# Fetching 31 of 1563 gather tiles of one graph layer row by row on SyncE and ScalarE

## The chip, the cores and the metric

The kernel runs on one core of one Trainium2 chip. The metric is the device time of one execution in microseconds, less being better. The time before is the median of three runs.

## The reference

Four graph layers over 12,500 nodes with 128 features and 200,000 edges sorted by destination. Each layer ends in a layer norm. The change is in the third layer (called "sum" in the kernel):

```python
x = _layernorm(x + L0(x, edges))          # softmax over edges
x = _layernorm(x + L1(x, src, dst))       # four attention heads, MLP
# the third layer, L2:
deg  = segment_sum(ones_like(dst), dst)   # self loops included
dinv = rsqrt(deg)
h    = x @ W
msgs = h[src] * (dinv[src] * dinv[dst])[:, None]
out  = gelu(segment_sum(msgs, dst) + b)
x = _layernorm(x + out)
# the fourth, L3: messages from gelu([x[src], x[dst], w] @ We1 + be1) @ We2
x = _layernorm(x + L3(x, edges, edge_weight))
```

## The kernel before

The edges are cut into 1563 tiles of 128 edges. Four tiles make a group (391 groups) and 16 tiles a block `b`. Each layer is one pass over the tiles, followed by a pass over the nodes. `edge_soft` runs the first layer (its tiles are named `rows`, `frow_h`) and the second (`rows_h`). `edge_light` runs the third, with mode "sum" (`rows_sum`, `pn_sum`), and the fourth, with mode "mlp" (`rows_mlp`, `frow_mlp`).

A tile needs the 128 rows of a table in DRAM that its edges' sources name. The usual way is one indirect DMA on GpSimd (L581 in `edge_light`), which picks the 128 rows by a column of indices and puts one into each partition of `rows`. There are eight group slots in `rows` (`NR`), so GpSimd may be at most eight groups, 32 tiles, ahead of the tensor engine; for slot reuse it waits on `s_mm`, which the last matmul of a group raises.

In "sum" mode the tensor engine's `place(g)` clears a PSUM bank with a matmul of zeros (L627), waits for the group's one-hot matrices `S` and for its gathered rows, and multiplies each tile's rows with its one-hot matrix (L640), which adds the rows of equal destinations. VectorE makes the one-hots one group ahead (`hot`, L745) and adds the PSUM bank into the accumulator `big` (`add`, L772), waiting for `s_mm`. A bank is used again only after the add of the group two before (`s_add`). ScalarE has nothing to do in this pass. SyncE loads some weights, writes a list of row addresses (`far_d`, then `flist`), writes `deg`, and is then idle.

There is a second way to bring in a tile, used for a few of them and called a lane: 128 separate DMAs of one row each, with the address of each read from `flist` into a register (`load_values`, 16 rows at a time). They fill `frow`, which has three slots (`DEEP`). In "mlp" mode lane 1 brings in the last tile of every sixth block on the ScalarE queue, 15 tiles, six rows after each activation. The first layer brings in 14 tiles the same way on the SyncE queue, one tile's 128 rows in one go (`fetch` in `edge_soft`, L941). GpSimd skips such tiles (`continue`).

```python
lanes = ([], FETCHED[1] if mlp else [])
lane = {t: (q, k) for q, tiles in enumerate(lanes) for k, t in enumerate(tiles)}
```

so that in "sum" mode `lane` is empty and GpSimd gathers all 1563 tiles.

Of the kernel before, what the change touches and what calls it, by code (L numbers as in the profile page):

```python
# [23 lines left out]
P = 128  # L24
# [8 lines left out]
NB = 16  # L33
# [7 lines left out]
SIZE = [min(4, TILES - 4 * g) for g in range(GR)]  # L41
# [3 lines left out]
SEED = 1597463007.0  # L45
RING = 8
APART = 6
FETCHED = ([], [NB * b + NB - 1 for b in range(6, 96, APART)])
DEEP = 3
FETCHED0 = [NB * b + NB - 1 for b in range(9, 90, APART)]  # L50
W0, W1, XR = F + 1, H * DH + H + 1, F + 8
# [11 lines left out]
def prog(nc, a, out, stop=99, debug=False):  # L63
    kind = "ExternalOutput" if debug else "Internal"

    def dram(name, shape, dt):
        return nc.dram_tensor(name, shape, dt, kind=kind).ap()
# [14 lines left out]
    deg_d = dram("deg_d", (NT, 3, P), BF16)  # L82
    far_d = dram("far_d", (sum(map(len, FETCHED)), P), I32)
    lrn_d = dram("lrn_d", (NT, P), BF16)

    with ExitStack() as top:
        def sb(name, shape, dt=F32, ctx=top):
            return ctx.enter_context(nc.sbuf_tensor(name, shape, dt))
# [55 lines left out]
        if stop <= 3:  # L144
# [5 lines left out]
            ("one3", [3, P], BF16))}  # L150
        consts["flist"] = sb("flist", [33, max(map(len, FETCHED)) * P], I32)
        edge_light(nc, sb, "sum", t2_d, big, dict(consts, dn=dn, w=w, a=a), d)
# [300 lines left out]
def edge_light(nc, sb, mode, table, acc, c, d):  # L453

    mlp = mode == "mlp"
    NR, NS, ND, NW = RING, 4, 4, 2
    PE, DVE, SP = mybir.EngineType.PE, mybir.EngineType.DVE, mybir.EngineType.SP
    NQ = NB // 4

    with ExitStack() as ctx:  # L460
# [8 lines left out]

        rows = s("rows", [P, NR, 4, F])  # L470
        idx, lr, regs = c["idx"], c["lr"], c["regs"]
        lanes = ([], FETCHED[1] if mlp else [])
        lane = {t: (q, k) for q, tiles in enumerate(lanes) for k, t in enumerate(tiles)}
        S = s("S", [P, NS, 4, P])
        zb = s("zb", [P, 512], BF16)
# [2 lines left out]
        if mlp:  # L478
            lrb = s("lrb", [P, NW, EB], U8)
            w = s("w", [P, B, NB])  # L480
            crowb = s("crowb", [P, F])
            dw = s("dw", [P, ND, 4, F])
            ST = s("ST", [P, 2, 4, P])
            pre = [ps(f"pre{i}", [P, 4, P]) for i in range(2)]
            s_base = sem("s_base")
            s_edge = [sem(f"s_edge{i}") for i in range(NW)]
            s_dw = [sem(f"s_dw{i}") for i in range(ND)]
            s_st, s_ex, s_pre, s_gelu = sem("s_st"), sem("s_ex"), sem("s_pre"), sem("s_gelu")
        else:
            we2, we2T = s("we2", [P, F]), s("we2T", [P, F])  # L490
            be2, be9, betc, buc = s("be2", [P, 1]), s("be9", [P, 9]), s("betc", [P, 1]), s("buc", [P, 1])
            bu2, be3 = s("bu2", [3, F]), s("be3", [3, F])
            v9, v9r, v9p = s("v9", [9, F]), s("v9r", [9, F]), s("v9p", [9, 3, F], BF16)
            mask, degf, deg = s("mask", [9, 6]), s("degf", [NT, P]), s("deg", [NT, 3, P], BF16)
            pw = ps("pw", [P, 4, P])
            s_w, s_dd, s_p, s_pv = sem("s_w"), sem("s_dd"), sem("s_p"), sem("s_pv")
            many = [len(tiles) for tiles in FETCHED]
            fcol, fidx = s("fcol", [P, sum(many)]), s("fidx", [sum(many), P], I32)
            px = ps("px", [P, P])
            s_fx = sem("s_fx")  # L500
# [3 lines left out]
        s_g, landed = c["s_g"], list(c["landed"])  # L504
        s_init, s_S, s_mm, s_add = sem("s_init"), sem("s_S"), sem("s_mm"), sem("s_add")
        block = ctx.enter_context(nc.Block(no_gpsimd_drain=True))
# [6 lines left out]
        def rows_of(e, engine, q, k, p, n):  # L513

            r0 = load_values(nc, engine, flist[32 * q:32 * q + 1, k * P + p:k * P + p + n], N * F * 4)
            for i in range(n):
                e.dma_start(frow[q][p + i:p + i + 1, k % DEEP, :].bitcast(U8), byte[:, bass.ds(r0[i], F * 4)]
                            ).then_inc(s_far[q][k % DEEP], 16)

        def gathered(g):  # L520
            return s_g[g % NR], landed[g % NR] + 16 * sum(near(k) for k in range(g % NR, g + 1, NR))
# [4 lines left out]
        @block.sync  # L526
        def _(e):
            if not mlp:
                a, wt = c["a"], c["w"]
                row = lambda n, k: a[n].rearrange("(o f) -> o f", o=1).broadcast_to([k, F])  # L530
                col = lambda n: a[n].rearrange("(p o) -> p o", o=1)
                e.dma_start(we2[:, :], a["L3_gnn_We2"]).then_inc(s_w, 16)
                e.dma_start(wt["wu"][:, :, :], a["L3_gnn_Wu1"].rearrange("(k p) j -> p k j", p=P)).then_inc(s_w, 16)
                e.dma_start(wt["we"][:, :, :], a["L3_gnn_We1"][0:2 * F, :].rearrange("(k p) j -> p k j", p=P)).then_inc(s_w, 16)
                e.dma_start(wt["wu2"][:, :], a["L3_gnn_Wu2"]).then_inc(s_w, 16)
                e.dma_start(wt["wg"][:, :], a["L2_gnn_W"]).then_inc(s_w, 16)
                e.dma_start(wt["bg"][:, :], row("L2_gnn_b", P)).then_inc(s_w, 16)
                for t, n in ((be2, "L3_gnn_be2"), (betc, "L3_gnn_beta"), (buc, "L3_gnn_bu1")):
                    e.dma_start(t[:, :], col(n), allow_slow_non_contiguous=True).then_inc(s_w, 16)
                for t, n, k in ((wt["be"], "L3_gnn_be1", P), (wt["bet"], "L3_gnn_beta", P), (wt["gam"], "L3_gnn_gamma", P),  # L540
                                (bu2, "L3_gnn_bu2", 3), (be3, "L3_gnn_beta", 3)):
                    e.dma_start(t[:, :], row(n, k)).then_inc(s_w, 16)
                e.wait_ge(s_fx, 3)
                e.dma_start(d["far"], fidx[:, :]).then_inc(s_dd, 16)
                e.wait_ge(s_dd, 16)
                for q in range(2):
                    if many[q]:
                        e.dma_start(flist[32 * q:32 * q + 1, 0:many[q] * P],
                                    d["far"][q * many[0]:q * many[0] + many[q], :].rearrange("t e -> (t e)").rearrange("(o x) -> o x", o=1)
                                    ).then_inc(s_dd, 16)  # L550
                listed = 16 + 16 * sum(n > 0 for n in many)
                e.wait_ge(s_dd, listed)
                e.wait_ge(s_pv, 3)
                e.dma_start(d["deg"], deg[:, :, :]).then_inc(s_dd, 16)
                e.wait_ge(s_dd, listed + 16)
                return
            e.dma_start(crowb[:, :], c["crow"].broadcast_to([P, F])).then_inc(s_base, 16)
            e.dma_start(w[:, :, :].rearrange("p b t -> p (b t)"), d["wcol"]).then_inc(s_base, 16)
            for g in range(GR):
                b, q = divmod(g, NQ)  # L560
                if q == 0:
                    if b >= NW:
                        e.wait_ge(s_ex, (b - NW + 1) * NQ)
                    e.dma_start(lrb[:, b % NW, :], d["lrrow"][b:b + 1, :].broadcast_to([P, EB])).then_inc(s_edge[b % NW], 16)
                    r0 = load_values(nc, SP, regs[BASE:BASE + 1, b * NB:(b + 1) * NB], N)
                if g >= ND:
                    e.wait_ge(s_ex, g - ND + 1)
                for j in range(SIZE[g]):
                    e.dma_start(dw[:, g % ND, j, :], d["dst"][bass.ds(r0[4 * q + j], P), :]).then_inc(s_dw[g % ND], 16)

        @block.gpsimd
        def _(e):
            for g in range(GR):
                if g >= NR:
                    e.wait_ge(s_mm, g - NR + 1)
                b, q = divmod(g, NQ)
                for j in range(SIZE[g]):
                    t = 4 * q + j
                    if 4 * g + j in lane:
                        continue  # L580
                    e.indirect_dma_start(rows[:, g % NR, j, :], None, table,  # L581
                                         bass.IndirectOffsetOnAxis(ap=idx[:, b, t:t + 1].bitcast(I32), axis=0)
                                         ).then_inc(s_g[g % NR], 16)

        if mlp:
            @block.scalar
# [72 lines left out]
        def _(e):  # L659
# [5 lines left out]
            e.memset(zb[:, :], 0.0)  # L665
            e.drain().then_inc(s_init, 1)
            if not mlp:
                for q in [q for q in range(2) if many[q]]:
                    f0, f1 = q * many[0], q * many[0] + many[q]
                    b0 = FETCHED[q][0] // NB  # L670
                    e.tensor_scalar(fcol[:, f0:f1], idx[:, b0:b0 + APART * (many[q] - 1) + 1:APART, NB - 1].bitcast(I32), float(F * 4), None, ALU.mult)
                e.drain().then_inc(s_fx, 1)
                e.wait_ge(s_fx, 2)
# [111 lines left out]
            for i in range(GR + lag):  # L785
# [8 lines left out]
                g = i - lag  # L794
# [5 lines left out]
                add(g, r0[g % 16])  # L800
            e.drain()

    for k in range(len(FETCHED[1]) if mlp else 0):
        c["far"][k % DEEP] += 16 * P
    for g in range(GR):
        c["landed"][g % NR] += 16 * sum(not mlp or 4 * g + j not in FETCHED[1] for j in range(SIZE[g]))


CHAIN = ("score", "scoreT", "scan1", "row1", "scanI", "col1", "scan2", "row2", "scanJ", "col2", "scan3", "exp",
# [1692 lines left out]
```

## Time and profile before

| | |
|---|---|
| median of 3 runs | 10216.46 us (10213.39 to 10222.34) |
| profiled execution, its own time | 10213.39 us |
| its span, first to last instruction | 10211.6 us |
| GpSimd (POOL) busy | 6159.7 us, 60% |
| TensorE matmul (PE) busy | 5172.9 us, 51% |
| VectorE (DVE) busy | 5157.6 us, 51% |
| ScalarE (ACT) busy | 2350.8 us, 23% |
| mean granted TensorE clock | 0.673 |

The span holds four edge passes one after the other, each with a node pass behind it. The pass that the change touches goes from the first gather into `rows_sum` at 5334.8 us to the last add into `big` at 7567.3 us. A share of the whole span therefore says little; what counts is what paces this pass.

### The profile page before, as it was taken

The page shows a single profiled execution, that of the slowest core. Times are in us where ns is not written, and L with a number is a line of the kernel's source. Part 1 is how long each engine was busy: PE and PEld are TensorE (multiplying, and loading weights), DVE is VectorE, ACT ScalarE, POOL GpSimd, SP SyncE. Part 2 cuts the span into 40 slices and gives each one's busy share as a digit, 9 for nine tenths or more (in the row PEclk, how much of TensorE's full clock was granted, in tenths as well). Part 3 has the DMA queues.
Part 4 walks back from the last instruction along what each step waited for, and adds up shares of the span by engine and source line. Part 5 has one row for each costly group of instructions (what it writes and reads, how often), then busy time and mean ns, then how long its engine had stood idle before and what let it go on. Part 6 is the DMA issues. An engine that isn't in the chain of part 4 may idle for free. (4 is left out here: it accounts for less than half of the span.)

```text
span 10211.6 us, 117807 instructions
## 1 busy us (share of the span) xinstructions
PE 5172.9 (51%) x26943; PEld 4434.7 (43%) x27385; DVE 5157.6 (51%) x11737; ACT 2350.8 (23%) x7991; POOL 6159.7 (60%) x6684
## 2 busy tenths in 40 slices
PE   1544444447365666666673323333345565666655
PEld 1434433435254555555552222222244555555553
DVE  4644544546466666666652222222245555555556
ACT  1212211224244444444460000000021111111114
POOL 5666666662566555555516666666656666666664
PEclk9556556667677777777786656555576766666677
DMA  4222222222444444444421111111123333333331
GB/s 110 46 46 47 46 46 46 47 46 86 100 101 99 99 98 98 98 98 98 99 68 47 46 47 46 47 46 46 46 62 109 100 101 101 102 100 102 101 100 43
DMA packets 869663, 769.76 MB, mean 75 GB/s; under 512 B 385028, under 2 KB 727929, under 8 KB 868606
## 3 DMA queue, kind: packets, MB, share of 16 engines
q0 software_dynamic: 230416, 528.66, 20.4%
q1 hardware_dynamic: 626235, 228.48, 9.4%
q10 hardware_dynamic: 12344, 5.06, 0.2%
q8 instruction: 255, 4.18, 0.2%
q14 instruction: 413, 3.38, 0.1%
HBM read 707.24 MB, written 54.30 MB: 75 GB/s over the span
## 5 line engine op out<-in xcount | busy, mean ns | idle before, releaser
L1007 POOL DMA_INDIRECT rows_h<-t_d,idx x1563 | 1482.3, 948 | 1024.9 <-issue 396.3
L581 POOL DMA_INDIRECT rows_sum<-t_d,idx x1563 | 1474.7, 944 | 962.8 <-issue 453.5
L581 POOL DMA_INDIRECT rows_mlp<-t_d,idx x1548 | 1468.7, 949 | 834.1 <-remote 419.0
L1007 POOL DMA_INDIRECT rows<-t_d,idx x1477 | 1396.7, 946 | 812.6 <-issue 409.7
L1152 PEld LDWEIGHTS pn_h<-S_h,rows_h 128*128 128x128 f32 x6252 | 1098.1, 260 | 258.5 <-issue 223.2
L1152 PE MATMUL pn_h<-S_h,rows_h 128*128 128x128 f32 x6252 | 1141.6, 348 | 124.8 <-issue 110.3
L1047 ACT ACTIVATE rows_h<-rows_h,wc_h 128x64 f32<-128x64 f32 x4688 | 1135.9, 334 | 17.1 <-issue 7.0
L772 DVE TENSOR_TENSOR big<-big,pn_sum 128x512 f32 x391 | 269.2, 689 | 1687.0 <-remote 1535.6
L620 PE MATMUL pre_mlp<-dw_mlp,ST_mlp 128*128 128x128 f32 x3126 | 674.5, 379 | 475.8 <-DVE ST_mlp L59 185.3
L627 PE MATMUL pn_sum<-zb_sum 128*128 128x512 bf16 x325 | 175.4, 540 | 1294.4 <-DVE big L772 1089.9
L620 PEld LDWEIGHTS pre_mlp<-dw_mlp,ST_mlp 128*128 128x128 f32 x3126 | 591.2, 280 | 528.5 <-issue 513.8
L1152 PE MATMUL pn_h<-S_h,rows 128*128 128x128 f32 x3126 | 736.3, 398 | 51.8 <-ACT rows L1047 20.5
L640 PE MATMUL pn_mlp<-S_mlp,rows_mlp 128*128 128x128 f32 x3126 | 664.6, 383 | 175.2 <-DVE big L772 96.1
L640 PE MATMUL pn_sum<-S_sum,rows_sum 128*128 128x128 f32 x3126 | 606.5, 358 | 236.1 <-DVE big L772 156.8
L591 ACT ACTIVATE rows_mlp<-rows_mlp 128x512 f32<-128x512 f32 x391 | 246.2, 630 | 2079.2 <-DVE rows_mlp L765 1335.3
L1152 PEld LDWEIGHTS pn_h<-S_h,rows 128*128 128x128 f32 x3126 | 683.6, 301 | 86.1 <-issue 44.9
L627 PEld LDWEIGHTS pn_sum<-zb_sum 128*128 128x128 bf16 x391 | 43.3, 111 | 1536.2 <-DVE big L772 1278.1
L640 PEld LDWEIGHTS pn_mlp<-S_mlp,rows_mlp 128*128 128x128 f32 x3126 | 655.7, 296 | 59.2 <-issue 14.6
L1161 PE MATMUL hist<-lo_h,ho_h 128*98 128x128 bf16 x1563 | 241.5, 305 | 771.1 <-DVE lo_h L1387 589.6
L640 PEld LDWEIGHTS pn_sum<-S_sum,rows_sum 128*128 128x128 f32 x3126 | 588.5, 271 | 66.7 <-issue 30.7
L772 DVE TENSOR_TENSOR big<-big,pn_mlp 128x512 f32 x391 | 269.1, 688 | 681.6 <-remote 629.6
L1463 DVE TENSOR_TENSOR acc<-acc,pn_h 128x512 f32 x391 | 269.4, 689 | 676.1 <-remote 521.9
(361 smaller groups left out, 8634.5 us busy)
## 6 DMA issues: line engine op xcount, KB each, us to landing
dw_mlp<-bd_d SPq DMA_DIRECT2D x1563, 64.0 KB
frow_mlp<-t_d ACTq DMA_DIRECT2D x1920, 0.5 KB
frow_h<-t_d SPq DMA_DIRECT2D x1792, 0.5 KB
lrb_h<-lrrow_d SPq DMA_DIRECT2D x196, 128.0 KB
lrb_mlp<-lrrow_d SPq DMA_DIRECT2D x98, 256.0 KB
rows_h<-t_d,idx POOLq DMA_INDIRECT x1563
dw_h<-xp_d SPq DMA_DIRECT2D x1563, 3.0 KB
rows_sum<-t_d,idx POOLq DMA_INDIRECT x1563
```

Of the source, the lines that this page charges most:

```text
L581: e.indirect_dma_start(rows[:, g % NR, j, :], None, table, bass.IndirectOffsetOnAxis(ap=idx[:, b, t:t + 1].bitcast(I32), axis=0)).then_inc ...
L591: e.activation(v, v, ACT.Gelu).then_inc(s_gelu, 1)
L620: last = e.matmul(pre[g % 2][:, j, :], ST[:, g % 2, j, :], dw[:, g % ND, j, :], start=True, stop=True)
L627: e.matmul(pn[g % 2][:, :], zb[:, 0:P], zb[:, :], start=True, stop=False)
L640: last = e.matmul(pn[g % 2][:, bass.ds(r0[j], P)], x, S[:, g % NS, j, :], start=False, stop=(j == SIZE[g] - 1))
L772: e.tensor_tensor(w, w, pn[g % 2][:, :], ALU.add).then_inc(s_add, 1)
L1007: e.indirect_dma_start(rows[:, g % NR, j, :], None, table, bass.IndirectOffsetOnAxis(ap=idx[:, b16, t:t + 1].bitcast(I32), axis=0)).then_i ...
L1047: last = e.activation(v, x, ACT.Copy, scale=wc[:, b % 2, t * heads + h:t * heads + h + 1])
L1152: last = e.matmul(pn[g % 2][:, k, bass.ds(r0, P)], rows[:, g % NR, j, k * P:(k + 1) * P], S[:, g % NS, j, :], start=False, stop=last_tile)
L1161: last = e.matmul(hist[:, :], ho[:, g % 2, j, :], lo[:, g % 2, j, :], start=False, stop=False)
L1463: e.tensor_tensor(w, w, pn[g % 2][:, :, :], ALU.add).then_inc(s_add, 1)
```

## The change

In "sum" mode 31 tiles leave GpSimd. Lane 0 (the last tile of blocks 3, 9, ..., 93, 16 tiles) is issued on the SyncE queue, lane 1 (blocks 6, 12, ..., 90, 15 tiles) on the ScalarE queue, each tile as 128 DMAs of one row. A lane issues its first three tiles without a wait, and from then on waits until the tile three before has been placed. In "mlp" mode lane 1 stays as it was. The list of addresses grows from 15 to 31 rows.

```diff
-FETCHED = ([], [NB * b + NB - 1 for b in range(6, 96, APART)])
+FETCHED = ([NB * b + NB - 1 for b in range(3, 96, APART)], [NB * b + NB - 1 for b in range(6, 96, APART)])
@@ edge_light
-        lanes = ([], FETCHED[1] if mlp else [])
+        lanes = ([], FETCHED[1]) if mlp else FETCHED
...
-            many = [len(tiles) for tiles in FETCHED]
+            many = [len(tiles) for tiles in lanes]
...
+        def fetch(e, engine, q):
+            for k, t in enumerate(lanes[q]):
+                if k >= DEEP:
+                    e.wait_ge(s_mm, lanes[q][k - DEEP] // 4 + 1)
+                for p in range(0, P, 16):
+                    rows_of(e, engine, q, k, p, 16)
@@ sync, after the weights, the list and deg
+                fetch(e, SP, 0)
@@ new
+        if not mlp and many[1]:
+            @block.scalar
+            def _(e):
+                e.wait_ge(s_dd, 48)
+                fetch(e, mybir.EngineType.Activation, 1)
@@ vector, the list of addresses
-                for q in [q for q in range(2) if many[q]]:
+                for q in range(2 if many[1] else 1):
...
-                    b0 = FETCHED[q][0] // NB
+                    b0 = lanes[q][0] // NB
@@ counts of landed DMAs for the later stages
-    for k in range(len(FETCHED[1]) if mlp else 0):
+    for k in range(0 if mlp else len(FETCHED[0])):
+        c["come"][k % DEEP] += 16 * P
+    for k in range(len(FETCHED[1])):
         c["far"][k % DEEP] += 16 * P
```

## Rows read from the trace of the kernel before

**Rows 1.** Span of the core, mean granted clock.

```profile
core 0: 10211.6 us, clock 0.673
```

**Rows 2.** Costliest groups: line, engine, operation, count, busy, mean ns, idle before, releaser.

```profile
L581 POOL DMA_INDIRECT rows_sum<-t_d,idx x1563 | 1474.7, 944 | 962.8 <-issue 453.5
L772 DVE TENSOR_TENSOR big<-big,pn_sum 128x512 f32 x391 | 269.2, 689 | 1687.0 <-remote 1535.6
```

**Rows 3.** Windows, sum and mlp pass: busy PE, PEld, DVE, ACT, POOL; clock, DMA share, GB/s.

```profile
5340.00:7550.00 2210.00, 683.54 (x3408) 610.71 (x3473) 505.27 (x812) 0.00 (x0) 1464.92 (x1553) 0.60 0.18 47
7700.00:9980.00 2280.00, 1365.77 (x6388) 1242.17 (x6516) 1320.01 (x3088) 241.31 (x383) 1453.25 (x1533) 0.67 0.38 101
```

**Rows 4.** The gather's line in the sum pass: durations, first and last start, idle before.

```profile
L581 POOL DMA_INDIRECT rows_sum<-t_d,idx x1563: 938/944/1061, 5334.8 to 7556.7; - x196
...
  issue: 453.5, 1478
  remote: 286.6, 75
```

**Rows 5.** Timeline of GpSimd: start, duration, idle before and its releaser.

```profile
5380.26 0.94 POOL L581 DMA_INDIRECT rows_sum<-t_d,idx  x1 [5.58 <-PE pn_sum L640]
...
6029.42 0.94 POOL L581 DMA_INDIRECT rows_sum<-t_d,idx  x1 [4.46 <-remote]
6030.67 0.94 POOL L581 DMA_INDIRECT rows_sum<-t_d,idx  x1 [0.30 <-issue]
```

**Rows 6.** GpSimd, mlp pass: tiles 87, 135, 183; then 1335, 1383, 1431.

```profile
7816.51 0.94 POOL L581 DMA_INDIRECT rows_mlp<-t_d,idx  x1 [0.30 <-issue]
...
7887.62 0.94 POOL L581 DMA_INDIRECT rows_mlp<-t_d,idx  x1 [0.30 <-issue]
...
7959.24 0.94 POOL L581 DMA_INDIRECT rows_mlp<-t_d,idx  x1 [0.30 <-issue]
...
9657.13 0.94 POOL L581 DMA_INDIRECT rows_mlp<-t_d,idx  x1 [0.30 <-issue]
...
9727.30 0.94 POOL L581 DMA_INDIRECT rows_mlp<-t_d,idx  x1 [0.30 <-issue]
...
9798.94 0.94 POOL L581 DMA_INDIRECT rows_mlp<-t_d,idx  x1 [0.30 <-issue]
```

**Rows 7.** SyncE's queue, first layer: one lane tile of 128 rows each.

```profile
406.78 85.15 SPq L941 DMA_DIRECT2D frow_h<-t_d  x128
...
1246.82 110.15 SPq L941 DMA_DIRECT2D frow_h<-t_d  x128
```

**Rows 8.** First layer's gathers in windows with and without SyncE issuing a lane tile.

```profile
1246.80:1356.00 109.20, 69.66 (x74) 0.61 0.21 46
1184.40:1246.80 62.40, 40.50 (x44) 0.58 0.21 47
1527.90:1634.10 106.20, 68.27 (x73) 0.61 0.21 46
1459.80:1527.90 68.10, 44.29 (x47) 0.58 0.21 47
```

**Rows 9.** SyncE's queue at the start of the sum pass.

```profile
5344.03 0.22 SPq L548 DMA_DIRECT2D flist<-far_d  x1
5349.22 0.31 SPq L554 DMA_DIRECT2D deg_d<-deg_sum  x1
```

**Rows 10.** Gather of tile 63, add of its group 15, first gather of group 23.

```profile
5423.14 0.94 POOL L581 DMA_INDIRECT rows_sum<-t_d,idx  x1 [0.30 <-issue]
...
5453.68 0.69 DVE L772 TENSOR_TENSOR big<-big,pn_sum 128x512 f32 x1 [0.73 <-issue]
...
5463.55 0.94 POOL L581 DMA_INDIRECT rows_sum<-t_d,idx  x1 [0.30 <-issue]
```

**Rows 11.** ScalarE around the sum pass, and its lane in the mlp pass.

```profile
7568.37 1.28 ACT L2148 ACT_TABLE_LOAD   x1 [2235.37 <-PEq L460]
...
7740.06 2.00 ACTq L517 DMA_DIRECT2D frow_mlp<-t_d  x6
```

More of the change, by code:

```diff
@@ L801, in _ @@
             e.drain()
-    for k in range(len(FETCHED[1]) if mlp else 0):
+    for k in range(0 if mlp else len(FETCHED[0])):
+        c["come"][k % DEEP] += 16 * P
+    for k in range(len(FETCHED[1])):
         c["far"][k % DEEP] += 16 * P
     for g in range(GR):
-        c["landed"][g % NR] += 16 * sum(not mlp or 4 * g + j not in FETCHED[1] for j in range(SIZE[g]))
+        c["landed"][g % NR] += 16 * sum(4 * g + j not in FETCHED[1] + ([] if mlp else FETCHED[0]) for j in range(SIZE[g]))
 CHAIN = ("score", "scoreT", "scan1", "row1", "scanI", "col1", "scan2", "row2", "scanJ", "col2", "scan3", "exp",
```

## The prediction

> **What bounds the kernel now.** I began with the span [rows 1] and the list of costliest groups [rows 2]. The largest are the indirect gathers of the four edge passes; that of the sum pass takes 944 ns of GpSimd each time. The change touches one pass only, so the share of the whole span is set aside and a window is laid over that pass [rows 3]: of 2210 us GpSimd is busy 1464.92, the matmuls 683.54, VectorE 505.27, ScalarE 0, and the DMA engines 0.18 of the time. Nothing in it is full. The DMA engines are not what is short: they move 47 GB/s here, and 101 GB/s in the mlp pass, which keeps GpSimd busy for nearly the same share [rows 3].
>
> The gather's own line [rows 4] gives the pace: first start 5334.8, last 7556.7, so (7556.7 - 5334.8) / 1562 = 1.4225 us from one to the next. It has two parts. Start to start inside a run of gathers is 1.25 us, as 6029.42 to 6030.67 shows [rows 5]: 0.94 busy and 0.30 that nothing else ends (1.249 in the mean over such pairs). The rest is pauses: 75 waits that another engine ended, 286.6 us together [rows 4], of the kind at 6029.42 with 4.46 us [rows 5]. They come mostly after 24 gathers: 24 x 1.249 = 29.97, plus 4.16 more than the usual 0.30, makes a cycle of about 34.2 us. The wait in the code at that place is the one for a free slot of `rows`, that is for `s_mm` of the group eight before. So the pass is paced by GpSimd's issuing for 88% of the time (1.249 / 1.4225), and for 12% GpSimd has run its ring full and waits for the tensor engine. VectorE is waiting at the same time: 1535.6 us idle before `big<-big,pn_sum` are put down to the same unknown releaser [rows 2]. The add of group 15 starts 5453.68 - 5423.14 = 30.5 us after the group's last gather [rows 10], though the matmuls of a group are busy for 683.54 / 391 = 1.75 us [rows 3]. The trace does not tell why the ring is used to its end by an engine that is busy a third of the time, and this is where I can be wrong.
>
> **The change part by part.** *Removed:* 31 gathers on GpSimd. Price of one: at least the 1.25 us of issue. At most the whole 1.4225 if its share of the pauses goes too. The mlp pass shows which is nearer, for it has lane tiles already. Between the gathers of tiles 87 and 135, with lane tile 111 among them, 71.11 us pass, and over the next 48 tiles, all gathered, 71.62. At the end of the pass, between tiles 1335 and 1383, with lane tile 1359 among them, 9727.30 - 9657.13 = 70.17; over the next 48, 9798.94 - 9727.30 = 71.64. These are the first and the last of 14 such pairs [rows 6], with means 70.17 and 71.43, a difference of 1.26. That is one issue, and the pauses stay as they are. Both kinds of window have the lane's DMAs running, so this is the gain without the lane's price. 31 x 1.249 = 38.7 us.
>
> *Added on the two queues:* 31 x 128 = 3968 row DMAs with their address registers, on SyncE and ScalarE. ScalarE is idle through the whole pass (2235.37 us before its next instruction, [rows 11]) and SyncE after 5349.22 [rows 9], so nothing is queued behind them there. What they may cost is felt by GpSimd or the tensor engine. The first layer shows such bursts: SyncE takes 85.15 us for a tile's 128 rows in one of the shortest of its 14 bursts and 110.15 in one of the longest, the first aside [rows 7]. In windows with a burst the gathers come every 109.20 / 74 = 1.476 and 106.20 / 73 = 1.455 us, in windows without one every 62.40 / 44 = 1.418 and 68.10 / 47 = 1.449 [rows 8]. The difference of the means, 1.465 - 1.434 = 0.031 us over the 70 gathers of a burst, would be 2.2 us per lane tile. This is an upper bound: the windows without a burst are the tail of a batch, where the softmax chain of that layer rests too. Lower bound: nothing, since the gathers of [rows 6] keep their 0.30 us of idle time although ScalarE issues rows in that pass, and the DMA share of 0.18 leaves room. I see no way to a gain from a burst. I take 0.25 us each, near the low end, because in this pass both issuing engines have nothing else to do and no chain is beside them: 31 x 0.25 = 7.8 us.
>
> The Trainium skill ("DMA: Bandwidth & Descriptors", Anatomy of one DMA) puts a fixed cost of about 2.0 us on each DMA, however small. If a lane paid that for each row in turn, a tile would take 128 x 2.0 = 256 us, as an estimate from that page, and the two lanes would be the bound of the pass. The bursts disagree as far as one lane goes: 85.15 / 128 = 0.67 and 110.15 / 128 = 0.86 us per row [rows 7], so the rows overlap in flight.
>
> *Can the lanes keep up?* Lane tiles of one lane are 96 tiles apart, and 96 tiles last 96 x 1.4225 = 136.6 us now, about 135 after the change. A burst takes 85 to 110. Both lanes run at once, which no stretch of this trace shows at full rate; ScalarE's six rows in 2.00 us [rows 11], issued while SyncE loads windows for the same pass, say that the two queues don't stand in line for each other. The tight one is the first: tile 63. SyncE can begin after 5349.22 + 0.31 [rows 9]; with 85 to 110 us it has issued the last row between 5435 and 5460, and the row lands a little later. VectorE adds its group now at 5453.68 [rows 10]. GpSimd asks for that group's slot at group 23, at 5463.55, so a tensor engine held until shortly after 5460 does not stop GpSimd: cost 0, and what is late beyond that is paid once. ScalarE's first, tile 111, has 48 tiles more to wait for, 68 us; the three slots put the others in time as long as a burst is under 135 us.
>
> *Added on VectorE and SyncE at the start:* one more small `tensor_scalar` for the list, and one more DMA for `flist` (0.22 us, [rows 9]). GpSimd stands still before its 33rd gather for 5.58 us until the first group's matmuls [rows 5], so VectorE's extra instruction goes straight into the path: about 0.3 us, from both sides between 0.1 and 1. I leave it out of the sum.
>
> *Moved:* nothing else. The waits of `place` on the lane's semaphore are new but met if the above holds; behind them stand the matmuls of the group, and behind those VectorE's add and GpSimd's slot.
>
> The sum: -38.7 + 7.8 = -31 us. Against the profiled execution's own 10213.4 us (span 10211.6, 1.8 around it) that is 10182.5; the median of the runs is 3.1 above that execution, so 10216.5 - 31 = 10185.5.
>
> **The rivals.** *The pauses take it back.* The tensor engine is a full ring behind, so it may be that some pace of its own, 34.2 us for six groups, rules the pass, and GpSimd only fills the time. For it: the 30.5 us of [rows 10], nearly the full ring, and VectorE's idle time. Against it: the pairs of [rows 6], where a ring of the same size paced GpSimd too. A cycle would stay at 34.2 us with 23 gathers and the pause 1.25 longer. Time 10216, no change.
>
> *The bursts cost more than a gather saves.* Place: the gather's pace, or the pause, while a lane issues. The lanes issue 31 x 97 = 3000 us in a pass of 2200, so somewhere a burst is always on. It decides from 1.25 us per burst, and is seen as slower from 1.9. At the 2.2 us from [rows 8]: 31 x 2.2 = 68, less 38.7, is 10246, slower. Against it: in [rows 8] the other work of the batch is mixed in.
>
> *The lanes are too slow together.* If two at once stretch a burst to 170 us, a lane needs 16 x 170 = 2720 us and the pass is 500 us longer. Stretched to 145, it is 16 x 145 = 2320 against 2190: 10290 or so. For it: a row DMA in [rows 7] takes two to three times the 0.33 us of [rows 11], so something already holds them up. Against it: 25 us to spare even at a long burst.
>
> *More than forecast:* a gather takes its share of the pause along and a burst is free. 31 x 1.4225 = 44 us: 10172. It lies in the same direction and is the low end.
>
> **How the numbers follow.** A difference of 0.2%, 20 us, is about what a measurement of this kernel can tell from none. The forecast with its own range (10170 to 10200) has 0.66, of which 0.03 stays within 20 us; pauses that take it back 0.17; costly bursts 0.12; slow lanes 0.05. That is faster 0.63, same 0.20, slower 0.17. The range goes from 10166, somewhat under the 44 us case, to 10232, which takes in the unchanged time and the lesser half of the costly bursts. It leaves out the slow lanes, the rest of the costly bursts, and 0.03 below.
>
> **What would show it.** 1532 gathers in `rows_sum` instead of 1563; start to start still 1.25 us; a cycle of six groups with a lane tile about 32.9 us long and one without 34.2; the sum of the pauses still near 280 us; last gather near 7526 instead of 7556.7; all other passes unchanged in length. If the pauses sum to 320 us, the first rival holds. If a lane's 128 rows take over 135 us and matmuls of `frow_sum` wait for DMAs, the lanes are too slow. If pauses grow in bursts only, it is their price. The weakest step is the 0.25 us; next to it that the rest of the ring behaves as in the mlp pass, whose pauses come after every 8 gathers and not after 24.

## The result: 0.9% slower

The median of the changed kernel is 10302.5 us (10276.5 to 10320.7) against 10212.8 us (10185.3 to 10222.3) for the kernel before, six runs each. The ratio is 1.0091 with a 95% interval of 1.007 to 1.011: 90 us slower by the medians, 93 (71 to 112) by the ratio. The prediction was 10185.5 us, 31 faster. The profiled execution took 10333.2 us itself, 31 above its median: the gathers of its first layer start at 158.4 us, those of the kernel before at 138.9. So lengths of passes are compared here and not their places in time.

The core's span, which answers to [rows 1], and the two groups that answer to [rows 2], from the list of costliest groups (columns as there; the gather's line is now L590, the add's L787):

```profile
core 0: 10331.4 us, clock 0.675
```

```profile
L590 POOL DMA_INDIRECT rows_sum<-t_d,idx x1532 | 1447.9, 945 | 1086.3 <-issue 432.3
...
L787 DVE TENSOR_TENSOR big<-big,pn_sum 128x512 f32 x391 | 269.2, 688 | 1779.9 <-remote 1369.7
```

The gathers are 31 fewer and 27 us less busy, and GpSimd's idle time before them grew by 124 us. A window over the pass (columns as in [rows 3]; this one is 90 us longer):

```profile
5360.00:7660.00 2300.00, 734.27 (x3400) 658.42 (x3464) 502.98 (x808) 0.00 (x0) 1436.20 (x1521) 0.60 0.17 45
```

GpSimd, VectorE and the DMA engines are no fuller than before, and the DMA engines move 45 GB/s where they moved 47: the rows are not short of bandwidth. The granted clock is 0.60 in both windows, so the clock is not the cause either. The gather's own line shows the pass and where the idle time went (it answers to [rows 4]; the row of POOLq is the stretch before the pass):

```profile
L590 POOL DMA_INDIRECT rows_sum<-t_d,idx x1532: 939/945/961, 5354.4 to 7672.8; - x192
...
  issue: 432.3, 1403
  remote: 321.8, 113
  POOLq L1812: 214.9, 1
  PE pn_sum L655: 117.3, 15
```

From first to last gather 2318.4 us pass, where it was 2221.9 [rows 4]: 96.5 longer. The last row is the one that grew. In the same view of the kernel before it was this:

```profile
  PE pn_sum L640: 8.0, 9
```

GpSimd waited 8.0 us for matmuls in this pass; now it waits 117.3, 15 times. What the matmuls wait for is seen at the lane's tiles, `frow_sum`:

```profile
L517 SPq DMA_DIRECT2D frow_sum<-t_d x2048: 2/228/1454, 5370.6 to 7625.8; - x187
L517 ACTq MOVE frow_sum<-t_d x1920: 3/29/1435, 5366.2 to 7254.6; - x192
L517 ACTq DMA_DIRECT2D frow_sum<-t_d x1920: 3/214/1417, 5366.3 to 7256.0; - x192
...
its engine sat idle before it (us, times) until:
  issue: 289.7, 17
  DMA frow_sum<-t_d: 262.6, 15
who waited for it (us, times):
  PE pn_sum L655: 274.1, 16
  DVE big L787: 197.7, 15
  POOL rows_sum L590: 109.6, 14
```

Fifteen times a matmul waits for a lane's rows, 262.6 us in all, and 109.6 us of that reach GpSimd through its ring of eight groups. The lane is SyncE's. In its timeline one row covers the whole pass, because nothing but row DMAs comes between:

```profile
5370.64 2255.89 SPq L517 DMA_DIRECT2D frow_sum<-t_d  x2048
```

That is 2255.89 / 16 = 141.0 us for a tile, against 85 to 110 in [rows 7] and the 135 to 137 that the pace allows. ScalarE's 15 tiles end at 7256.0, 417 us before the last gather, at 126 us each with its waits for slots.

The first of the waits is tile 63, the one that the prediction called tight. First the matmuls of its group, then GpSimd at group 23, in their timelines:

```profile
5469.80 0.50 PE L655 MATMUL pn_sum<-S_sum,rows_sum 128*128 128x128 f32 x3
5509.52 0.79 PE L655 MATMUL pn_sum<-S_sum,frow_sum 128*128 128x128 f32 x2 [39.23 <-DMA frow_sum<-t_d]
```

```profile
5510.58 0.94 POOL L590 DMA_INDIRECT rows_sum<-t_d,idx  x1 [26.01 <-PE pn_sum L655]
5511.83 0.94 POOL L590 DMA_INDIRECT rows_sum<-t_d,idx  x1 [0.31 <-issue]
```

The row arrives 139 us after SyncE began, and GpSimd stands for 26 us. Start to start after it is 1.25 us, as before. The passes around changed much less: from first to last gather 2490.1 us in the second layer (2503.8 before) and 2309.7 in the mlp pass (2300.7).

### The profile page after: what moved, and what is told of

Read it like the earlier page. It is cut to its first block and busy times, and to the rows that moved or that the text cites. A ratio compares the mean times of both kernels' runs of the same rounds, so it can differ in the third digit from the quotient of the medians.

```text
span 10331.4 us, 125962 instructions
## 1 busy us (share of the span) xinstructions
PE 5216.4 (50%) x26943; PEld 4473.0 (43%) x27385; DVE 5156.8 (50%) x11738; ACT 2353.7 (23%) x7991; POOL 6140.1 (59%) x6653
## 5 line engine op out<-in xcount | busy, mean ns | idle before, releaser
L590 POOL DMA_INDIRECT rows_sum<-t_d,idx x1532 | 1447.9, 945 | 1086.3 <-issue 432.3
L590 POOL DMA_INDIRECT rows_mlp<-t_d,idx x1548 | 1469.2, 949 | 842.5 <-remote 426.4
L787 DVE TENSOR_TENSOR big<-big,pn_sum 128x512 f32 x391 | 269.2, 688 | 1779.9 <-remote 1369.7
L655 PE MATMUL pn_sum<-S_sum,rows_sum 128*128 128x128 f32 x3064 | 632.2, 375 | 258.3 <-issue 126.1
L655 PEld LDWEIGHTS pn_sum<-S_sum,rows_sum 128*128 128x128 f32 x3064 | 626.5, 290 | 73.7 <-issue 31.5
L787 DVE TENSOR_TENSOR big<-big,pn_mlp 128x512 f32 x391 | 269.0, 688 | 678.3 <-remote 618.3
```

The costliest lines, as they stand in the source:

```text
L590: e.indirect_dma_start(rows[:, g % NR, j, :], None, table, bass.IndirectOffsetOnAxis(ap=idx[:, b, t:t + 1].bitcast(I32), axis=0)).then_inc ...
L655: last = e.matmul(pn[g % 2][:, bass.ds(r0[j], P)], x, S[:, g % NS, j, :], start=False, stop=(j == SIZE[g] - 1))
L787: e.tensor_tensor(w, w, pn[g % 2][:, :], ALU.add).then_inc(s_add, 1)
```

## The experiments

All stand against the kernel before on their own chip. In the tables, "idle" is the sum of GpSimd's three rows of idle time in this pass (issue, remote, matmuls of `pn_sum`), 748.1 us in the kernel before [rows 4, with 8.0 for the matmuls]. Each gather that is gone would take 0.305 us of it along (1.249 - 0.944); "more" is what is above that. "About us" is the difference from the kernel before: the ratio, less one, times its median. A "burst" is the 128 row DMAs of one lane tile.

How far can one trace's idle time be trusted? Two later runs, `mlp_plain` and `no_lanes`, leave this pass as it was, and have 750.3 and 746.4 us of it. In the mlp pass, which 13 of the traces share unchanged, it goes from 825.0 to 841.5. So "more" is good to some 5 us, and 24 us over 15 bursts is 1.6 us each, give or take 0.4.

### What the pieces cost: one lane, no lane, no use of the rows

`left_out`: the 31 tiles are neither gathered nor fetched (their matmuls read a cleared buffer, so their edges' messages are missing).

```diff
-                fetch(e, SP, 0)
-                fetch(e, mybir.EngineType.Activation, 1)
```

> The 31 tiles are neither gathered nor fetched: zeros stand in for their rows, so the third layer lacks these 3968 edges. What 31 gathers are worth with no price. Theories A and B: 31 x 1.25 to 1.42 = 39 to 44 us faster than before. Theory C: within 10 us of before, the pauses longer by 39 us in sum.

`act_only`: SyncE's lane empty, its tiles gathered. `sp_only`: the same for ScalarE's.

```diff
-        lanes = ([], FETCHED[1]) if mlp else FETCHED
+        lanes = ([], FETCHED[1])                     # act_only
+        lanes = ([], FETCHED[1]) if mlp else (FETCHED[0], [])   # sp_only
```

> ScalarE's lane alone: its 15 tiles are fetched row by row in the sum pass, the 16 of SyncE's lane are gathered again. Theory A (SyncE's lane is the bound: it needs some 141 us for a tile's 128 rows where its tiles are 96 x 1.42 = 137 us apart, and the gathers are not slowed): ScalarE's bursts of 97 to 132 us fit in, so 15 gathers at 1.25 us are saved, 19 us faster than before, about 10194. Theory B (each burst slows the gathers; the changed kernel's 90 us and the 39 us saved, over 31 tiles, make 4.2 us per burst): 15 x (4.2 - 1.25) = 44 us slower. Theory C (the pauses take back what is saved): no change.

> SyncE's lane alone: 16 tiles, ScalarE's 15 are gathered again. Theory A: as slow as both lanes if a burst still takes 141 us (16 x 141 + 55 us = 2311 us of pass against 2232, 75 to 95 us slower than before); if SyncE is slow only because ScalarE issues beside it, bursts fall to 100 us and the kernel is 20 us faster than before. Theory B: 16 x (4.2 - 1.25) = 47 us slower.

`rows_unused`: all 1563 tiles gathered, both lanes' 3968 row DMAs issued all the same.

```diff
-        lane = {t: (q, k) for q, tiles in enumerate(lanes) for k, t in enumerate(tiles)}
+        lane = {...the same...} if mlp else {}
+                    e.wait_ge(s_far[q][k % DEEP], before[q][k % DEEP] + 16 * P * (k // DEEP))
```

> All 1563 tiles are gathered, and both lanes' 3968 row DMAs are issued all the same; the tensor engine reads the gathered tiles and waits for no row. Price of the bursts alone. Theory A: the gathers keep their 1.42 us, first to last 2222 us; the pass ends only when SyncE has issued its last row, at some 16 x 141 us, 60 us later than before. Theory B: first to last gather takes 31 x 4.2 = 130 us more.

`act_unused`: `rows_unused` with ScalarE's lane alone.

> All 1563 tiles are gathered as before; ScalarE issues its 15 x 128 row DMAs all the same, and no one uses them; SyncE has none. This is the price of a burst by itself. At 1.5 us each the kernel is 15 x 1.5 = 22 us slower than before (+15 to +30) and the pauses of the pass are near 271.7 + 22 = 294 us. At the forecast's 0.25 us it would be +4 us, at 2.2 us +33.

| | gathers | bursts | ratio (95%) | about us | idle | more |
|---|---|---|---|---|---|---|
| left_out | 1532 | 0 | 0.996 (0.9945 to 0.9974) | -41 | 732.3 | -6 |
| act_only | 1548 | 15 | 1.0007 (0.9998 to 1.0016) | +7 | 766.0 | +22.5 |
| sp_only | 1547 | 16 | 1.0026 (1.0014 to 1.0038) | +27 | 783.4 | +40 |
| act_unused | 1563 | 15 | 1.0033 (1.0022 to 1.0044) | +34 | 772.2 | +24 |
| rows_unused | 1563 | 31 | 1.0199 (1.0173 to 1.0224) | +203 | 793.5 | +45 |
| changed kernel | 1532 | 31 | 1.0091 (1.007 to 1.011) | +93 | 871.4 | +133 |

The gathers are worth what was forecast, 41 us for 31. The price of a burst is not: 22.5 / 15 = 1.5 us by idle time in `act_only`, 24 / 15 = 1.6 in `act_unused`, and (7 + 18.7) / 15 = 1.7 and 34 / 15 = 2.3 by the ratios. The rows that show it, the same view as above, of `act_unused`:

```profile
L596 POOL DMA_INDIRECT rows_sum<-t_d,idx x1563: 942/947/981, 5337.9 to 7587.5; - x196
...
  issue: 444.6, 1456
  remote: 320.5, 103
...
  PE pn_sum L661: 7.1, 3
```

Nobody uses or waits for these rows, and still the row "remote" went from 286.6 to 320.5 us. Its count alone (75 to 103) proves little: in `mlp_plain` and `no_lanes`, where this pass is as before, it reads

```profile
  remote: 291.4, 73
```

```profile
  remote: 291.5, 90
```

A steadier count is that of gathers that start more than 2.25 us after the one before: 69 in the kernel before, 67 and 66 in these two, 97 in `act_unused`. The median from start to start stays at 1.25 us. The extra time also ends with the bursts: up to the gather of tile 1300, where ScalarE's last row (7204.1) has just been issued, `act_unused` needs 1877.9 us and the kernel before 1848.4; for the 262 tiles after it 371.6 and 373.5.

`act_unused` was expected at +15 to +30 us and came out at +34, a little above. None of the three theories written down for `act_only` (19 us faster, 44 slower, no change because pauses take the saving back) named a price of this size. The measured "no change" is the saving and the price cancelling, for `left_out` shows that the pauses take nothing back. `sp_only` also fell between its theories. Its 40 us are mostly waiting. Two rows of the view of its lane tiles, matmuls waiting for rows and GpSimd waiting in turn:

```profile
  DMA frow_sum<-t_d: 108.1, 10
...
  POOL rows_sum L592: 36.4, 6
```

SyncE needs (7543.3 - 5359.5) / 16 = 136.5 us for each tile there, all that the pace allows: even alone it has nothing to spare.

`rows_unused` is far slower for another reason, and by more than was written down for it (+203 us against some 60): its gathers are over at 7596.0, and SyncE is still issuing until 7771.9. That tail is a measurement in itself. Rows that SyncE issued, first in 200 us with both lanes and the gathers running, then in 150 us after the last gather (count; shortest, median and longest duration in ns; first and last start):

```profile
L519 SPq DMA_DIRECT2D frow_sum<-t_d x147: 3/287/1408, 6000.0 to 6199.7; - x147
...
L519 SPq DMA_DIRECT2D frow_sum<-t_d x366: 227/228/265, 7600.0 to 7749.9; - x183
```

A row takes 200 / 147 = 1.36 us beside the gathers and the other lane, and 150 / 366 = 0.41 us alone: 174 and 52 us for a tile. The gathers themselves are charged 45 us for the 31 bursts, 1.5 us each, although both lanes run together until ScalarE's ends at 7430.5.

### What slows the lanes: gathers, the other queue, instructions

`no_gathers` (one run): the changed kernel with no gather in this pass; the 1532 other tiles multiply a cleared buffer.

```diff
-            for g in range(GR):
+            for g in range(GR if mlp else 0):
```

> GpSimd gathers nothing in the sum pass; the tensor engine multiplies zeros in place of the 1532 gathered tiles and the 31 fetched ones as before. The layer's result is left out. If it is the gathers that hold up the row DMAs, a burst takes some 51 us on both queues, as SyncE's last three did once the gathers were over in the run with unused rows; the pass then lasts 16 x 52 = 830 us or less. If the two queues hold up each other, bursts stay over 80 us. Groups before the first lane tile show the tensor engine's own pace: under 2 us a group if it too is only held up by the gathers.

`swap`: SyncE brings in ScalarE's 15 tiles and the reverse.

```diff
-                fetch(e, SP, 0)
+                fetch(e, SP, 1)
-                fetch(e, mybir.EngineType.Activation, 1)
+                fetch(e, mybir.EngineType.Activation, 0)
```

> Both lanes as in the change, but the 16 tiles go over ScalarE's queue and the 15 over SyncE's. ScalarE's bursts were shorter (114 us against 140). If that belongs to the engine's queue, the 16 tiles now come in time and SyncE's 15 are the late ones, which end one tile sooner: about 15 x 141 us of issuing, 60 to 90 us slower than before. If it belongs to the list or the buffer, the bursts swap too, and the time is that of the change, 90 us slower.

`fixed_rows`: each row DMA has a fixed address, so it needs no register; other rows than the edges name are brought in.

```diff
-            r0 = load_values(...)
+            x = (k * P + p + i) * F * 4
+            e.dma_start(frow[...], byte[:, x:x + F * 4]).then_inc(s_far[q][k % DEEP], 16)
```

> As the change, but the row DMAs have fixed addresses: no register loads and no address arithmetic, so other rows than the edges' are added for the 31 tiles. The same 3968 DMAs and bytes, about a quarter of the instructions. If the queues' instructions are what gathers hold up (gaps came in steps of 0.71 us, as if per instruction), a burst falls to 40 to 60 us, nobody waits for a lane, and with the price of a burst halved or less the kernel is 15 to 40 us faster than before. If it is the DMAs themselves, bursts stay at 100 to 140 us and it is 50 to 90 us slower than before.

Without gathers (8856.9 us in one run) both queues run at the free rate at once. In 200 us of `no_gathers`, SyncE and ScalarE:

```profile
L519 SPq DMA_DIRECT2D frow_sum<-t_d x486: 227/228/360, 5599.9 to 5799.9; - x162
...
L519 ACTq DMA_DIRECT2D frow_sum<-t_d x483: 213/214/505, 5600.1 to 5798.8; - x161
```

The same stretch of time in `sp_only`, `act_only` and `fixed_rows`, gathers running:

```profile
L519 SPq DMA_DIRECT2D frow_sum<-t_d x194: 2/228/737, 5999.4 to 6199.2; - x194
```

```profile
L519 ACTq DMA_DIRECT2D frow_sum<-t_d x210: 2/213/1421, 6002.1 to 6199.2; - x105
```

```profile
L519 SPq DMA_DIRECT2D frow_sum<-t_d x238: 2/252/1388, 5999.8 to 6199.8; - x119
```

So the gathers take SyncE's queue from 486 rows to 194, and ScalarE's lane on top of them to 147 (above): 132 us for a tile alone and 174 with the other. (The 194 are from a stretch in which the pass waits for the lane now and then, which helps the lane, as `late0` shows below.) The two lanes do not touch each other when there are no gathers. With fixed addresses SyncE gets 238 rows done in the stretch although it rests between tiles, and nothing waits for a lane: the kernel is faster than before, 0.9976 (0.9966 to 0.9986), with an idle time of 762.3, 24 more than due and not 133. The pass itself is 11 us shorter (2210.8 against 2221.9); the rest of the 25 us by the ratio lies elsewhere or is scatter. Both the rate and the price get better; 24 / 31 = 0.8 us for a burst. The bursts take 56 to 75 us on ScalarE, near the 40 to 60 expected, and 66 to 88 on SyncE. Two things changed at once, though: a row needs fewer instructions, and the rows now lie one behind the other in the table. Which of the two helps, no run here separates.

`swap` is at 1.0074 (1.0054 to 1.0094). SyncE, now with 15 tiles, needs (7502.5 - 5334.1) / 15 = 145 us for each and makes the matmuls wait 243.4 us (14 times); ScalarE with 16 takes 121. The slow one is SyncE's queue and not the one or the other list.

```profile
L519 ACTq DMA_DIRECT2D frow_sum<-t_d x2048: 2/214/1409, 5330.4 to 7271.7; - x187
...
L519 SPq DMA_DIRECT2D frow_sum<-t_d x1920: 2/228/1417, 5334.1 to 7502.5; - x192
```

### Price or wait: lanes with time to spare

`sp_half`: every second tile on SyncE (8), all 15 on ScalarE. `late0`: all but tile 63 (15 and 15). `half_half`: every second of both (8 and 8, without tile 63).

```diff
+USE = (range(0, 16, 2), range(15))      # sp_half
+USE = (range(1, 16), range(15))         # late0
+USE = (range(1, 16, 2), range(0, 15, 2))   # half_half
-        lanes = ([], FETCHED[1]) if mlp else FETCHED
+        lanes = ([], FETCHED[1]) if mlp else tuple([FETCHED[q][i] for i in USE[q]] for q in range(2))
```

> SyncE's lane takes every second of its tiles (8 instead of 16), ScalarE's all 15; 1540 tiles are gathered. Reading so far: the pass of the changed kernel is 96 us longer because 31 gathers save 39, each burst costs 1.5 us more of pauses (46), and waiting for SyncE's 141 us per tile costs the other 86 to 90. If so, SyncE now has 270 us per tile, no matmul waits for a lane row, and 23 x (1.5 - 1.25) = 6 us are left: 10212, no change. Rival (two lanes at once hurt each other or the gathers more than the sum of one and one): 30 us slower or more.

> As the changed kernel, but tile 63, the first of SyncE's lane, is gathered again: 1533 gathers, 15 bursts on SyncE. A tile in 140 us is too slow only if the first one is asked for early; with tile 159 as the first, SyncE has one burst's time in hand (first asked for at about 5570, rows there at 5510), and 15 x 140 = 2100 us fits into the pass. If waiting for lane tiles is what made the changed kernel slow, this one is at about +30 x (1.5 - 1.25) = +8 us against the kernel before (+0 to +25), with matmuls waiting for lane DMAs under 20 us in all and pauses near 271.7 + 30 x 1.5 = 317 us. If instead two lanes together cost the pass more than one by one (2.9 us for each burst and more, whatever is waited for), it stays at +60 to +90 us, with pauses near 400.

> Every second tile of each lane: 8 on SyncE (tile 159 the first), 8 on ScalarE, the others gathered again. 1547 gathers, 16 bursts, each lane with 270 us for a tile, so that nothing waits for one. Theory (a burst has a price of about 1.8 us wherever it is issued, and what the changed kernel pays beyond that is waiting for SyncE's lane): 16 x (1.8 - 1.25) = +9 us (0 to +20), no matmul waits for a lane DMA, GpSimd's waits for pn_sum under 10 us. Rival (two lanes that run at once cost more than one, waiting or not): a burst costs 3 us or more, and it is +28 us or more.

| | bursts | ratio (95%) | about us | idle | more | of it, matmuls |
|---|---|---|---|---|---|---|
| sp_half | 23 | 1.0024 (1.0014 to 1.0034) | +25 | 788.5 | +47 | 29.2 |
| late0 | 30 | 1.0062 (1.0048 to 1.0076) | +63 | 827.2 | +88 | 79.4 |
| half_half | 16 | 1.0005 (0.9996 to 1.0014) | +5 | 767.2 | +24 | 7.7 |

`sp_half` was expected at no change and came out at +25: one matmul waited for a lane all the same, 34.4 us for tile 63, of which 21.1 reached GpSimd. Without that its 47 us are 26 for 23 bursts, 1.1 each.

`half_half` is the clean one: two lanes in play for two thirds of the pass (until 6761.7 and 6860.2), no wait for a lane, and 24 / 16 = 1.5 us for a burst, as with one lane. By the ratio it is (5 + 20) / 16 = 1.6. With the 1.5 of `rows_unused`, nothing points to a price that two lanes at once have beyond this.

```profile
L592 POOL DMA_INDIRECT rows_sum<-t_d,idx x1547: 938/944/1058, 5341.9 to 7567.6; - x194
...
  issue: 440.4, 1444
  remote: 319.1, 100
...
  PE pn_sum L657: 7.7, 2
```

`late0` went against what I expected of it. I had taken SyncE's 140 us as the speed of its queue, which with one burst in hand would have been enough. It is not a speed but where the pass settles. SyncE in `late0`, early, when it is not waited for, and later, when it is; and the first time that GpSimd waits for its tile:

```profile
L519 SPq DMA_DIRECT2D frow_sum<-t_d x155: 3/228/1412, 5400.0 to 5598.7; - x155
...
L519 SPq DMA_DIRECT2D frow_sum<-t_d x193: 3/228/1449, 6000.5 to 6199.9; - x193
```

```profile
6034.60 0.95 POOL L592 DMA_INDIRECT rows_sum<-t_d,idx  x1 [12.63 <-PE pn_sum L657]
```

While GpSimd gathers at its full pace the queue issues 155 rows in 200 us, a tile in 165; that is over the 137 between two of its tiles, and the head start is used up at 6034. From then on GpSimd stands still for some us at most lane tiles, and the queue gets to 193. SyncE's first four bursts take 159 to 177 us, all later ones 132 to 141; in `rows_unused`, where nobody waits, the first twelve take 162 to 188. That the queue gains because fewer gathers run while GpSimd stands still is the likely reason, not one that a run isolates. Leaving out tile 63 saved 93 - 63 = 30 us against the changed kernel, not far from the 26 of its one wait, though each of the two figures is uncertain by 15 to 20. `late0` did not remove the lane's waits, as I wrote it would; `half_half` did.

### Is it this pass alone? The lanes that were there before

`mlp_plain`: the kernel before, the mlp pass's lane taken out (1563 gathers there). `no_lanes`: the first layer's as well.

```diff
-        lanes = ([], FETCHED[1] if mlp else [])
+        lanes = ([], [])
-        lane = {} if gat else {t: k for k, t in enumerate(FETCHED0)}
+        lane = {}                                # no_lanes
```

> The kernel before with the one lane of the mlp pass taken out too: 1563 gathers there instead of 1548, and no row DMAs on ScalarE. If 15 bursts cost there what they cost in the sum pass, 1.5 us each against 1.25 saved, this is the same or 4 us faster than before. If the bursts are free in that pass, where ScalarE hands them out six rows at a time, it is 15 x 1.25 = 19 us slower.

> The kernel before with no lane anywhere: the mlp pass without its 15 tiles on ScalarE (which by itself gave 0.9985) and the first layer without its 14 on SyncE; their tiles are gathered. If a burst has the same price of 1.5 to 2.2 us in the first layer as elsewhere, against 1.25 saved, it is another 3 to 13 us faster than with the mlp lane alone taken out: -18 to -28 us against the kernel before. If a row burst on SyncE is free there, it is 14 x 1.25 = 17 us slower than that: about 0.

Both beat the kernel before, by 15 and 17 us: `mlp_plain` 10193.7 us, 0.9985 (0.9973 to 0.9997), and `no_lanes` 10186.8 us, 0.9983 (0.9974 to 0.9992). For `mlp_plain` at most 4 us had been expected. The mlp gathers of `mlp_plain`, and then of the kernel before, whose group [rows 6] shows single tiles of:

```profile
L581 POOL DMA_INDIRECT rows_mlp<-t_d,idx x1563: 938/944/1186, 7678.3 to 9968.6; - x196
...
  issue: 417.7, 1367
  remote: 394.4, 195
```

```profile
L581 POOL DMA_INDIRECT rows_mlp<-t_d,idx x1548: 938/944/1192, 7690.9 to 9991.6; - x194
...
  remote: 419.0, 197
  issue: 412.0, 1349
  PE pn_mlp L640: 2.2, 1
```

Fifteen more gathers, and the pass is 2290.3 us long where it was 2300.7. The idle time is 812.1, 25.7 less than the 837.8 due: 1.7 us for a burst there too, though ScalarE hands its rows out six at a time. It is no accident of one trace: the pass takes 2295.6 to 2309.7 us in the 13 traces that have its lane, 2290.3 and 2287.3 in the two without. In the first layer 14 more gathers leave the pass as it was (138.0 to 2311.4, before 138.9 to 2313.0), so a burst costs about what a gather does. The scatter of that pass between traces, 2169.7 to 2182.7 us, leaves room for 1.0 to 1.9 us, and by the ratios `no_lanes` and `mlp_plain` are not told apart.

## Why the prediction was wrong

- **31 x 1.249 = 38.7 us saved:** right. `left_out` measured 41 (27 to 56). The pauses stayed (285.8 us in the row "remote", 286.6 before), as taken from the pairs of [rows 6], so the rival that has them rule the pass fell.
- **0.25 us for a burst:** the first failed step, a term off in size. It measured 1.5 to 2.3 us with one lane and 1.5 to 1.6 with two, 31 x 1.5 = 47 us in place of 7.8. The bound of 2.2 from [rows 8] was near the truth, and the reasons that I gave for the low end were none: that both issuing engines have nothing else to do does not bear on what their rows do to GpSimd's gathers, and the pairs of [rows 6] compare stretches with bursts with stretches with bursts, so they could only show the saving. I said so and then leaned on their 0.30 of idle time. The price sits in the pauses, not in the usual gap.
- **"The lanes keep up":** the second failed step, and the one that makes the change slow. The rate was taken from [rows 7], a pass whose gathers have the same pace (1.42 to 1.48 us, [rows 8]) but where no other lane runs; 85 to 110 us there, 132 for SyncE alone in this pass, 165 to 174 with ScalarE's lane, and 141 in the changed kernel, where the pass waits for it. The tile is wanted every 137. "ScalarE's six rows in 2.00 us" [rows 11] was no evidence: it is one of the quick groups of six, near the free rate. GpSimd gathers there too, and the very next group of six in the same trace takes nearly twice as long:

```profile
7744.49 3.89 ACTq L517 DMA_DIRECT2D frow_mlp<-t_d  x6
```

- **The first tile, 63, in time:** wrong. Its rows took until 5509.5, not 5435 to 5460: 26 us of wait, once. The trace of the kernel before had a warning. I took 85 to 110 us from its bursts with "the first aside", and gave no reason for that; the first burst was the longest by 20 us, and tile 63 is a first one too (139 us):

```profile
165.95 128.98 SPq L941 DMA_DIRECT2D frow_h<-t_d  x128
```

- **One more list DMA and `tensor_scalar`:** 0.3 us was left out of the sum, and nothing in these runs could show it.

The sum with measured terms: -39 for the gathers, +47 to 50 for the bursts, and the rest of the 133 us of new idle time, some 85, for the waits, gives 94 us; measured were 93 (71 to 112). That the sum comes out checks only the 39 and the 133, for the waits are what is left over. How the 133 divide between price and waits is open within bounds. The trace of the changed kernel gives GpSimd 109.6 us of waiting for lane rows, which leaves 23 for the price; the price of the other runs asks for 47. A wait for a lane probably swallows pauses that would have come anyway. Either way the larger part is waiting. The rival "the lanes are too slow together" was right in place, mechanism and nearly in size: it spoke of 170 us for a stretched burst where 174 was found, and gave 10290 for 145. (By its own terms, 2320 - 2190 = 130 us more on top of 10185.5, it should have said 10315.) It put all on the two lanes together, while SyncE's lane had no time to spare even alone. It had a chance of 0.05. Its 500 us for 170 did not come, because the lane got faster once the pass waited for it (174 us against 141). The costly bursts (0.12, 10246) held as well, and the two add up.

The Trainium skill ("DMA: Bandwidth & Descriptors", Issuing engines are not separate DMA queues) says that transfers started on several engines interleave on the same 16 DMA engines, and that starting them on more engines saves only the time to initiate them, usually small beside the transfer. In this case the time to initiate is not small: the DMA engines are busy 0.17 of the window, and the time from one row's issue to the next rises from 0.41 us to 1.36. The 2.0 us that the prediction takes from the same page stand in a section on DMAs issued by GpSimd, while the lanes' rows are issued by SyncE and ScalarE; no burst here comes near the 256 us worked out from it, the longest is 188.

What stays open: what it is in the gathers that holds up the two queues, and why the groups' matmuls and adds run so far behind the gathers (without gathers, at a granted clock of 0.85 around these rows, the adds follow each other every 1.49 us, as the two rows of VectorE in `no_gathers` below show, while with them an add comes 30.5 us after its gather, [rows 10]), why SyncE's queue is slower than ScalarE's, and slower alone here (132 us for a tile) than in the first layer, and whether the price comes from the row transfers or from the register loads beside them; `fixed_rows` keeps the transfers and drops the loads, but changes which rows are read.

```profile
5422.20 0.69 DVE L788 TENSOR_TENSOR big<-big,pn_sum 128x512 f32 x1 [0.20 <-issue]
5423.69 0.69 DVE L788 TENSOR_TENSOR big<-big,pn_sum 128x512 f32 x1 [0.20 <-issue]
```

## What to carry to other kernels

Work that is moved off a busy engine is not free because the new engine is idle: price it by a run that adds it and takes nothing away (here `act_unused`), before counting the saving. A rate read in another pass holds only with the same neighbours; where two helpers are each near their limit alone, ask for the rate of both at once. And a saving measured with the helper running on both sides of the comparison says nothing of what the helper costs.

## What the runs showed of the hardware

- Row DMAs on SyncE and ScalarE take 0.41 us each while GpSimd issues no indirect gathers, and 0.95 to 1.36 beside them, at a DMA busy share of 0.17.
- Two lanes, which do not slow each other without gathers (486 and 483 rows in 200 us), do with them (SyncE 194 alone, 147 with ScalarE's).
- Rows at fixed addresses that follow each other, without register loads, are issued faster beside the same gathers (bursts of 66 to 88 us on SyncE, against 162 to 188) and disturb them half as much (0.8 us for 128, against 1.5). Whether the instructions or the addresses make the difference isn't shown.
- 128 unused row DMAs cost GpSimd's gathers 1.6 us of idle time, as more pauses (97 over 2.25 us from start to start, against 66 to 69) and not as a wider usual gap.
